# Attention on one core of Trainium2: first guess of the roots of q and k by ln and exp on ScalarE, one Newton step on VectorE

## The reference

```
h = _ln(x, ln1_g, ln1_b) + shift
qkv = (h @ Wqkv.T).reshape(b, n, 3, H, HD)
q = _ln(qkv[:, :, 0].transpose(0, 2, 1, 3), qn_g, qn_b)
k = _ln(qkv[:, :, 1].transpose(0, 2, 1, 3), kn_g, kn_b)
v = qkv[:, :, 2].transpose(0, 2, 1, 3)
scores = jnp.einsum('bhnd,bhmd->bhnm', q, k) / jnp.sqrt(jnp.float32(HD))
attn = jax.nn.softmax(scores, axis=-1)
o = jnp.einsum('bhnm,bhmd->bhnd', attn, v)
x = x + o.transpose(0, 2, 1, 3).reshape(b, n, H * HD) @ Wout.T
```

## Time and profile before

| | |
|---|---|
| median of three runs | 1519.02 us (1517.57 to 1520.0) |
| the profiled execution, its own time | 1515.56 us |
| its span, first to last instruction | 1513.7 us |
| TensorE busy | 1408.4 us, 93% of the span |
| VectorE busy | 1021.6 us, 67% |
| ScalarE busy | 961.4 us, 64% |
| GpSimd busy | 779.2 us, 51% |
| granted clock of TensorE, mean | 0.985 of full speed |
| first block, attention, experts | to about 335, 337 to about 1240, and the rest |

### The profile page before, as it was taken

One profiled execution on the slowest core, in us unless ns is written; L12 is line 12 of the kernel. 1 busy time (PEld: TensorE's weight loads), 2 busy tenths in 40 slices (PEclk: granted clock), 3 DMA queues, 4 the chain that ended last, 5 costly groups with the idle time before them and its releaser, 6 DMA issues. The chain is left out here.

```text
span 1513.7 us, 31706 instructions
## 1 busy us (share of the span) xinstructions
PE 1408.4 (93%) x9953; PEld 1158.5 (77%) x9953; DVE 1021.6 (67%) x2500; ACT 961.4 (64%) x2537; POOL 779.2 (51%) x736
## 2 busy tenths in 40 slices
PE   4799999997899999999999999999999887899997
PEld 3799999985577777777777777777777566799996
DVE  5866667635776776786777777677667658665652
ACT  4556665545778777777777777877877640345452
POOL 3576666643545645644654554564555430264633
PEclk9899999999999999999999999999999999999999
DMA  5341222110122212221221222221222236267652
GB/s 153 96 134 62 69 63 69 47 50 7 50 71 77 85 64 78 91 79 55 91 84 71 80 75 83 77 84 64 78 84 78 84 100 250 73 197 231 195 168 28
DMA packets 92412, 138.96 MB, mean 92 GB/s; under 512 B 8656, under 2 KB 61824, under 8 KB 92160
## 3 DMA queue, kind: packets, MB, share of 16 engines
q1 hardware_dynamic: 84032, 126.30, 24.7%
q0 software_dynamic: 6144, 8.39, 2.9%
q10 hardware_dynamic: 2112, 2.88, 0.6%
HBM read 87.20 MB, written 50.35 MB: 91 GB/s over the span
## 5 line engine op out<-in xcount | busy, mean ns | idle before, releaser
L1288 POOL TENSOR_TENSOR prob<-prob,share_p 128x512 f32<-128x512 f32 x256 | 268.1, 1053 | 326.4 <-DVE share_p L1391 326.4
L1197 ACT ACTIVATE prob<-bank,shift 128x256 f32<-128x256 f32 x512 | 236.0, 474 | 111.6 <-DVE shift L1385 111.4
L1385 DVE TENSOR_REDUCE shift<-bank 128x2 f32<-128x512 f32 x256 | 164.6, 684 | 193.5 <-PE bank L1058 188.6
L1283 POOL TENSOR_TENSOR raw_qk<-raw_qk,rq 128x512 f32<-128x512 f32 x128 | 145.5, 1149 | 67.1 <-DVE rq L100 67.1
L147 PE MATMUL bank<-wqkv_h,rowsT_h 128*128 128x512 f32 x384 | 160.8, 419 | 4.5 <-PEq L313 3.5
L1084 PE MATMUL bank<-pT,v 128*64 128x256 f32 x1024 | 139.6, 394 | 27.0 <-ACT pT L1260 27.0
L147 PE MATMUL bank<-wqkv_h,rowsT_l 128*128 128x512 f32 x384 | 152.4, 397 | 0.0
L147 PE MATMUL bank<-wqkv_l,rowsT_h 128*128 128x512 f32 x384 | 151.8, 395 | 0.0
L1058 PE MATMUL bank<-landing 64*128 64x256 f32 x1024 | 145.3, 402 | 3.1 <-ACT prob L1197 3.1
L1071 PEld LDWEIGHTS bank<-ident,prob 128*128 128x128 f32 x1024 | 109.4, 141 | 44.2 <-issue 41.8
L1071 PE MATMUL bank<-ident,prob 128*128 128x128 f32 x1024 | 140.8, 280 | 0.6 <-POOL prob L1288 0.3
(11 more groups left out here) (285 smaller groups left out, 4103.4 us busy)
## 6 DMA issues: line engine op xcount, KB each, us to landing
ew_raw<-in_fc1s SPq DMA_DIRECT2D x32, 256.0 KB, 3.2
split_w1h<-ew_h SPq DMA_DIRECT2D x32, 256.0 KB, 2.0
split_w1l<-ew_l SPq DMA_DIRECT2D x32, 256.0 KB, 2.5
ew_raw<-in_fc2s SPq DMA_DIRECT2D x32, 256.0 KB, 2.9
split_w2h<-ew_h SPq DMA_DIRECT2D x32, 256.0 KB, 2.1
split_w2l<-ew_l SPq DMA_DIRECT2D x32, 256.0 KB, 2.6
ew_h<-split_w1h SPq DMA_DIRECT2D x8, 1024.0 KB, 4.9
ew_l<-split_w1l SPq DMA_DIRECT2D x8, 1024.0 KB, 7.1
```

Of the source, the lines that this page charges most:

```text
L1197: last = nc.scalar.activation(prob[at][:, n, :], score_bank[side][:, n * T:(n + 1) * T], ACT.Exp, bias=shift[:, at, n:n + 1], scale=-1.0, ...
L1283: nc.gpsimd.tensor_tensor(part, part, rq[:, n, c * 8:(c + 1) * 8].unsqueeze(2).to_broadcast([P, 8, HD]), ALU.mult).then_inc(normed, 1)
L1288: nc.gpsimd.tensor_tensor(prob[at][:, :, :], prob[at][:, :, :], share[:, at, :].unsqueeze(2).to_broadcast([P, TT, T]), ALU.mult).then_inc( ...
L1385: nc.vector.tensor_reduce(shift[:, s % 2 * 2 + side, :], score_bank[side][:, :].rearrange("p (n m) -> p n m", n=TT), AX, ALU.min).then_inc ...
```

## The change

`chains` no longer calls `rsqrt_op`. VectorE makes mean plus eps one half slot earlier, in half slots 1 and 5 (the ends of pairs 0 and 2). ScalarE takes its logarithm and then exp(-0.5 x) of that as the first guess (`seeds`), in pairs 1 and 3, ahead of the exps of the pair. VectorE makes one Newton step of three operations at the start of pairs 1 and 3. `rooted` now counts both the mean and the final value. The wait for GpSimd to have used the old `rq` (`normed`) moves from VectorE to ScalarE's Exp. At the start of attention a set of functions with both logarithm and exp is loaded. The two semaphores of the output weights are now those of the first block, counted on, which changes no wait.

```
-SUM_SLOT, NORM_SLOT = (2, 6), (4, 8)
+MEAN_SLOT, SEED_PAIR, NORM_SLOT = (1, 5), (1, 3), (4, 8)
...
+        logs = sbuf(s, "logs", [P, 2 * H])
...
+                def seeds(b, n):
+                    wait(act, rooted, 2 * TT, b, 2 * n + 1)
+                    nc.scalar.activation(logs[:, :], ssq[:, n, :], ACT.Ln).then_inc(seeded, 1)
+                    wait(act, seeded, 2 * TT, b, 2 * n + 1)
+                    wait(act, normed, 8, b - 1, (n + 1) * QKC)
+                    nc.scalar.activation(rq[:, n, :], logs[:, :], ACT.Exp, scale=-0.5).then_inc(seeded, 1)
...
+                nc.scalar.preload_act_table_set("natural_log_exp_and_others")
                 nc.scalar.activation(flat(wo_h[:, :, :]), flat(o_raw), ACT.Copy).then_inc(wo_hi, 1)
...
+                        for n in range(TT):
+                            if live(t + 1) and s == SEED_PAIR[n]:
+                                seeds(t + 1, n)
                         if live(t):
                             exps(t, s)
...
-                                wait(pool, rooted, TT, b, n + 1)
+                                wait(pool, rooted, 2 * TT, b, 2 * n + 2)
...
-                        k = (i - SUM_SLOT[n]) * SPOTS + spot
-                        if live(new) and 0 <= k <= RSQRT_OPS:
-                            if k == 0:
-                                wait(dve, summed, 8, new, (n + 1) * QKC)
-                                link.note(nc.vector.tensor_scalar(ssq[:, n, :], ssq[:, n, :], 1.0 / HD, LN_EPS, ALU.mult, ALU.add))
+                        if live(new) and i == MEAN_SLOT[n] and spot == 0:
+                            wait(dve, summed, 8, new, (n + 1) * QKC)
+                            nc.vector.tensor_scalar(ssq[:, n, :], ssq[:, n, :], 1.0 / HD, LN_EPS, ALU.mult, ALU.add).then_inc(rooted, 1)
+                        if live(new) and i == 2 * SEED_PAIR[n] and spot < 3:
+                            y, v = rq[:, n, :], ssq[:, n, :]
+                            if spot == 0:
+                                wait(dve, seeded, 2 * TT, new, 2 * n + 2)
+                                link.note(nc.vector.tensor_tensor(rt[:, :], y, y, ALU.mult))
+                                continue
+                            link.settle()
+                            if spot == 1:
+                                link.note(nc.vector.scalar_tensor_tensor(rt[:, :], rt[:, :], -0.5, v, ALU.mult, ALU.mult))
                             else:
-                                if k == 1:
-                                    wait(dve, normed, 8, new - 1, (n + 1) * QKC)
-                                link.settle()
-                                ins = rsqrt_op(nc, k - 1, ssq[:, n, :], rq[:, n, :], rt[:, :])
-                                ins.then_inc(rooted, 1) if k == RSQRT_OPS else link.note(ins)
+                                nc.vector.scalar_tensor_tensor(y, rt[:, :], 1.5, y, ALU.add, ALU.mult).then_inc(rooted, 1)
...
-LINKS_ATTENTION = 60
+LINKS_ATTENTION = 24
```

More of the change, by code:

```diff
@@ L176, in build @@
         o_raw = landing[:, 3, :].rearrange("p (k n) -> p k n", n=D)
-        att_loaded, = sems(top, "att_loaded")
+        att_loaded, hi_done, lo_pool = sems(top, "att_loaded hi_done lo_pool")
         mid = top.enter_context(ExitStack())
@@ L193, in build @@
         first_block(nc, a, exponent, banks, ident, x1_rows, hbias, cols, target_rows, load_attention,
-                    (landing, qk_raw, v_raw, center, att_loaded), rows_of, sbuf, sems)
-        attention(nc, exponent, (landing, o_raw, wgate), rows_of, banks, ident, x1_rows, hbias, cols, x2_rows, logit,
+                    (landing, qk_raw, v_raw, center, att_loaded, hi_done, lo_pool), rows_of, sbuf, sems)
+        attention(nc, exponent, (landing, o_raw, wgate, hi_done, lo_pool), rows_of, banks, ident, x1_rows, hbias, cols, x2_rows, logit,
                   out, a, halves, sbuf, sems)
@@ L207, in first_block @@
 def first_block(nc, a, exponent, banks, ident, x1_rows, hbias, cols, target_rows, load_attention, weights, rows_of, sbuf, sems):
-    landing, qk_raw, v_raw, center, att_loaded = weights
+    landing, qk_raw, v_raw, center, att_loaded, hi_done, lo_pool = weights
     wq_h, wq_l, x_t, fold, fold_h, fold_l, stats, moment, var_eps, rstd, norm_sems = rows_of
@@ L906, in attention @@
 def attention(nc, exponent, weights, rows_of, banks, ident, x1_rows, hbias, cols, x2_rows, logit, out, a, halves, sbuf, sems):
-    landing, o_raw, wgate = weights
+    landing, o_raw, wgate, wo_hi, wo_lo = weights
+    FIRST_HI, FIRST_LO = 4, 1
     wq_h, wq_l, x1, aT, a_h, a_l, stats, moment, var_eps, rstd, norm_sems = rows_of
@@ L937, in attention @@
         (x1_again_in, tr_proj, tr_x2, tr_gates, tr_qk, out_proj, out_x2, out_gates, out_qk,
-         chunk_done, chunk_out, summed, rooted, normed, scored, lowest, exped, inverted, shared, pT_done, pT_act, pT_dve,
-         pv_done, o_hi, o_lo, x2_done, x2_stored, ew_in, ew_hi, ew_lo, ew_stored, out_spread, out_root, out_normed, x2n_stored, wo_hi, wo_lo, links) = sems(
+         chunk_done, chunk_out, summed, rooted, seeded, normed, scored, lowest, exped, inverted, shared, pT_done, pT_act, pT_dve,
+         pv_done, o_hi, o_lo, x2_done, x2_stored, ew_in, ew_hi, ew_lo, ew_stored, out_spread, out_root, out_normed, x2n_stored, links) = sems(
             s, "x1_again_in tr_proj tr_x2 tr_gates tr_qk out_proj out_x2 out_gates out_qk "
-               "chunk_done chunk_out summed rooted normed scored lowest exped inverted shared pT_done pT_act pT_dve "
-               "pv_done o_hi o_lo x2_done x2_stored ew_in ew_hi ew_lo ew_stored out_spread out_root out_normed x2n_stored wo_hi wo_lo att_links")
+               "chunk_done chunk_out summed rooted seeded normed scored lowest exped inverted shared pT_done pT_act pT_dve "
+               "pv_done o_hi o_lo x2_done x2_stored ew_in ew_hi ew_lo ew_stored out_spread out_root out_normed x2n_stored att_links")
         def first(b):
@@ L1090, in project @@
                     if first(b):
-                        pe.wait_ge(wo_lo, 1)
+                        pe.wait_ge(wo_lo, FIRST_LO + 1)
                     tr_free(pe, t, "proj", n)
@@ L1213, in empty @@
                         if isinstance(b, int) and b == 1:
-                            act.wait_ge(wo_lo, 1)
+                            act.wait_ge(wo_lo, FIRST_LO + 1)
                         dst, g = (qT, QN_G) if j % 4 < 2 else (kT, KN_G)
@@ L1289, in divide @@
                                             ALU.mult).then_inc(shared, 1)
-                pool.wait_ge(wo_hi, 1)
+                pool.wait_ge(wo_hi, FIRST_HI + 1)
                 nc.gpsimd.tensor_tensor(flat(wo_l[:, :, :]), flat(o_raw), flat(wo_h[:, :, :]).bitcast(F32), ALU.subtract).then_inc(wo_lo, 1)
```

4 lines of the change are left out of this document (2 added, 2 removed).

## The result

The change takes **1505.06 us** (median of 4 runs, 1504.29 to 1506.99) where the kernel before, run beside it, takes 1519.49 (1517.57 to 1520.0): a ratio of 0.9914, with a 95% interval of 0.9902 to 0.9926. By that ratio it is 13.1 us less, by the two medians 14.4.

What follows compares the result with a forecast made beforehand. TensorE bounds attention, so only its waits count, nearly all for ScalarE's copy of the transposed probabilities. Terms -9.4 - 2.6 + 1.3 = -10.7 us take the median from 1519.02 to 1508.3 us, range 1503 to 1517.

Steps and rivals of the forecast that it cites:

- What bounds the kernel, and the waits at pair 2: Attention steps 1 to 14: TensorE bounds, VectorE's order makes pair 2 wait; the wait goes whole, -9.4 us.
- What is late next is nothing there: Pair 2 in the steps: with its wait gone nothing else is late, pair 5 being the model.
- Step 0: Pair 2 of step 0: its 2.45 us come back whole, 0.15 more from the table load: together -2.6 us.
- ScalarE's cost: Ln and Exp ahead of the exps of pairs 1 and 3: 0.2 to 0.22 us each, 0.45 a pair, covered.
- GpSimd: Normalising of q and k: starts earlier without waiting; TensorE doesn't wait for it in steady state, so nothing.
- The start: Start of attention: the table load ahead of the split of `wout` lands whole on the path, +1.3 us (+0.3 to +1.5).
- The sum: Whole kernel: -9.4 - 2.6 + 1.3 = -10.7 us.
- Half stays: Rival: VectorE waits for Exp, the minimum of pair 2 stays late, about 6 us come back, 1514; chance 0.12.
- no change: Rival: the start and new small waits at pairs 1 and 3 eat the gains, 1517 to 1520; chance 0.08.
- Slower, ScalarE late: Rival: seeds make ScalarE late at pairs 1 and 3, slower from 1.4 us, 1537 at 2.0; chance 0.05.
- One table kept: Rival that it isn't: every Ln and Exp in attention reloads, about 1567 us; chance next to nothing.
- More, by shorter waits behind the jump: Rival: pair 0's waits after the loop's jump, at most 5 us together, shrink too, 1503; chance 0.03.

Runs made afterwards that it cites:

- (1): Kernel before with its root chain ended after the first Newton step, no Ln or Exp on ScalarE: 1506.49 us (0.9931).
- (6): The change with four Newton steps instead of one on the root of tile 0: 1519.53 us (1.0015).
- (7): The change with four Newton steps instead of one on the root of tile 1: 1504.92 us (0.9915).
- 12: The change without its Newton step, Exp's result being the root that GpSimd waits for: 1505.61 us (0.9919).
- the change again: The change unaltered, run and profiled a second time: 1505.74 us (0.9923).
- Experiment 8: The change with Ln issued nine times instead of once per tile, eight into a spare tile: 1510.59 us (0.9957).
- (3): The change with the table load one instruction later, behind the split of wout: 1504.4 us (0.991).
- 2: The change with the table load moved to the end of the first block, where ScalarE is idle: 1503.83 us (0.9914).
- (4): The change with two table loads in a row at the place of one: 1506.97 us (0.993).
- experiment 11: The change with only the first batch's seeds of tile 0 one chunk earlier, table load left in place: 1504.14 us (0.9908).
- experiment 5: The change with the table load in the first block's tail and the first batch's tile 0 seeds one chunk earlier: 1499.61 us (0.9881).

## Why the prediction was right, and where it was not

**What bounds the kernel, and the waits at pair 2: right.** -9.4 was said for steps 1 to 14; their pairs 2 are 9.30 us shorter: t=1 1.38 (1.4 said), even steps of the loop 0.91 on average (0.90), odd ones 0.44 (0.45), 12 to 14 0.41 (0.42). Adding 0.07 to each idle figure was right too. That it is the length of VectorE's chain in pair 1 is shown from both sides: shortened without ScalarE's help (1), the gain is there; made long again behind ScalarE's guess (6), it is gone; long in pair 3 (7), nothing happens.

**"What is late next is nothing there": right,** and 12 shows that nothing more was to be had. Pair 4, counted as nothing, gave 0.33 at step 14, where it had waited 0.24.

**Step 0: right in its cause, partly by luck in its size.** -2.6 was said and -2.57 read in the first trace: pair 0 -0.49, pair 1 +0.20 (the seeds ahead of its exps), pair 2 -2.14 (its wait falls from 4.65 to 2.51 us). The minimum there is still 1.48 behind its scores, not 1.16: the wait did not come back whole. And in the change again step 0 is 3.98 shorter, since the clock held behind the same wait; before and in the first trace it had fallen there.

**ScalarE's cost: right.** Two operations of 0.25 and 0.23 us (0.2 to 0.22 said), 0.5 a pair, covered. L99's 41.9 us went to 6.1 (L1353), further down than the two thirds said, since the slow place beside GpSimd is now hit by the product ahead of it (L1349, 623 ns). Experiment 8 bears the room at pair 1 out (0.95 said for even steps: with seeds of 0.5 + 0.96 = 1.46 they lose 0.53).

**GpSimd: right,** nothing, in the steps. At the start it is on the path.

**The start: the step that failed.** The prediction has "all of it lands on this path, +1.3", ends +0.3 and +1.5. Measured are 2.55 and 2.42, outside its ends. The load's 1.29 is right, the path too (3), and "the shorter chain gives little back here, since the seeds stand behind ScalarE's chunks" (2 shows 0.4). The term was too small because it held the wait alone and not TensorE's clock, which runs one stretch more at its lower level: with the load in the tail or behind the split the start is 39.4, with the load ahead of it 42.2 to 42.4 in three traces (7 among them), 2.9 for a load of 1.3. In the change again and in 7 that stretch follows a wait that the load made longer (3.14 and 3.12 us for 1.87); why it fell where it did in the first trace is open, and in experiment 11 (the early seeds alone) nothing came on top. The +2.7 that the page of the Trainium skill would give was near for another reason; the drain that it is made of is not there (4).

**The sum: 2.4 us too small a gain by the ratio, 3.7 by the medians, and 2.2 too large a one by the traces.** By the profiled pair it is -8.5 in the spans, for a predicted -10.7. The terms that it left out: the start's other 1.3; 2.1 more gained in steps 1 to 14 outside pair 2; 1.5 lost in step 15, where pair 0's values ran at the lower clock; 1.2 in the rest; 0.2 in the entry. They have both signs, so that the sum came as near as it did is in part luck. The rest goes with the clock too: it lasts 289.8 to 290.0 us in the four traces that spend 13 to 17 us of it at the lower level (before is one), and 290.4 to 293.0 in the ten that spend 21 to 26. The 2.1 is 0.02 to 0.05 us in nearly every pair (pairs 3, 4 and 6 of steps 2 to 13 last 6.86 on average instead of 6.89). It is there in every kernel with seeds and not in the one with the short chain alone (6.89), so it comes with the seeds and not with the chain's length. Its cause was not found. The scatter of the times did the rest: the forecast set the median 3.5 above the profiled run, as the runs before showed; the change's median lay 1.9 below its profiled run.

**The rivals.** *Half stays* and *no change*: no trace has them; VectorE's first Newton operation waits for Exp 3.3 us in 32 times, of which 2.73 is the very first. *Slower, ScalarE late*: the mechanism is real (8), the price was too high. The room at pair 3 was taken as that of pair 1, 0.93; the trace after shows 0.63 + 0.94 = 1.57 beyond the seeds, and at 1.46 us of seeds pair 3 lost nothing, where the rival's price has 0.53. The crossing lies above the 1.4 us given: at 1.46 the kernel is still 7 us below the one before. *One table kept*: right, no load other than those named is in attention. *More, by shorter waits behind the jump*: refuted. The minimum of pair 0 in step 4 comes 1.24 us behind its scores, 2.55 before, and TensorE's wait is 1.30 for 1.36. ScalarE is the late one there; after the jump it stood for 2.05 us with nothing to wait for that the trace shows:

```profile
592.96 0.38 ACT L1262 ACTIVATE o_h<-bank 128x256 fp32r<-128x256 f32 x1 [2.05 <-issue]
593.24 0.47 ACT L1199 ACTIVATE prob<-bank,shift 128x256 f32<-128x256 f32 x1
```

## What to carry to other kernels

An engine that is not the bottleneck sets the time where its in-order stream puts work with slack ahead of a short link that the bottleneck waits for: shorten the stream at that place, and expect the wait back and little more. A chain can move to an engine that idles ahead of its own next link, with the room read from two places, that idle time and the slack behind it; but read the prologue by itself, where the same chain has no cover. There its place among the chunks cost 1.4 us up to the normalising (experiment 5 against 2) and a table load ahead of a split that others wait for 1.3, and up to 1.7 more in single traces where TensorE's clock fell; without both the kernel was 2.8 us faster side by side. Put a table load into the last idle stretch before it is needed, across a block's boundary if that is where the stretch lies.

## What was not expected of the hardware

A wait of one and the same length in the same place, 2.51 us at pair 2 of step 0, sometimes lowered TensorE's clock and sometimes not. The values behind it in the change and with the load in the tail, and the windows that follow (granted clock before the DMA's share):

```profile
394.84 1.97 PE L1086 MATMUL bank<-pT,v 128*64 128x256 f32 x8 [2.51 <-ACT pT L1273]
...
395.00:396.00 1.00, 1.00 (x6) 0.50 0.00 0
```

```profile
392.28 1.08 PE L1087 MATMUL bank<-pT,v 128*64 128x256 f32 x8 [2.51 <-ACT pT L1273]
...
393.00:394.00 1.00, 1.00 (x10) 1.00 0.00 0
```

Eight matmuls take 1.97 us at 1.2 GHz or 1.08 at 2.4, and the pair 7.61 or 6.27. Of the ten traces with this wait of 2.51 us, three have 7.6, one 7.34 and six 6.27. In the change itself both lengths came. So at step 0 this is a scatter of 1.3 us, which no edit made and which a comparison of two single profiles takes for the edit's work.

The end of step 14 and pair 0 of step 15 are another matter. TensorE waits there 1.77, 1.77 and 2.2 us before and after alike. Pair 0 goes from 5.96 (before) to 7.31 (the change, both times), and where a variant shows 5.96, pairs 6 and 7 of step 14 are 1.0 to 1.3 us longer instead. All twelve traces whose pairs 2 no longer wait from step 2 on have one stretch at the lower clock around these pairs; the two whose pairs 2 wait (before, four Newton steps on tile 0) have none in steps 1 to 15. Where the stretch falls scatters; that there is one may belong to the gone waits. It takes 0.5 to 1.6 us of what they give, and its cause was not found.

The spread of the entry into attention is of the same size: 337.39 to 339.08 over the fourteen traces, though of all edits only the load in the tail lies ahead of it.
